# Routed sums of 48 row tiles on GpSimd instead of VectorE, with the last segment's first unit moved ahead

## What is computed

```python
x = L0_attn_a_x
x = x + _L0_attn_a_ref(_layernorm(x), ...)        # recurrence over 512 steps, 16 heads
x = x + _L0_ffn_ref(_layernorm(x), ...)           # experts
x = x + _L0_attn_b_ref(_layernorm(x), ...)        # causal attention
x = x + _L0_ffn_ref(_layernorm(x), ...)           # experts, same weights

# recurrence, one step for all sequences and heads
Sk = einsum('bhde,bhe->bhd', Sm, k_t)
Sm = Sm + beta_t[..., None] * einsum('bhd,bhe->bhde', v_t - Sk, k_t)
o_t = einsum('bhde,bhe->bhd', Sm, q_t)

# experts
scores = sigmoid(xt @ gate_w.T)
_, idx = lax.top_k(scores + gate_b, 4)
w = take_along_axis(scores, idx); w = w / sum(w) * 2.5
y = sum over the four chosen experts e of  w_e * (silu_and_mul(xt @ w13_e.T) @ w2_e.T)
y = y + silu_and_mul(xt @ w13_s.T) @ w2_s.T       # shared expert
```

## Time and profile before

| | us |
|---|---|
| median of 3 executions | 5779.35 |
| lowest and highest | 5775.86 and 5791.94 |
| the profiled execution, its own time | 5783.49 |
| the profiled execution, its span from first to last instruction | 5782.3 |

### The profile page before, as it was taken

The page is one execution under the profiler, slowest core; times in us unless marked ns, Lnnn a source line. Parts: engine busy times, 40 slices in busy tenths (PEclk is TensorE's granted clock), DMA queues, the critical chain, the costliest instruction groups (busy, mean ns, idle before and its releaser), DMA issues.

```text
span 5782.3 us, 71376 instructions
## 1 busy us (share of the span) xinstructions
PE 3420.9 (59%) x20276; PEld 2403.0 (42%) x20372; DVE 4123.7 (71%) x10439; ACT 1976.3 (34%) x4743; POOL 1764.7 (31%) x2760
## 2 busy tenths in 40 slices
PE   6312053663436533263548878876788778877664
PEld 3101031452315422152435555543565555545554
DVE  1999989999899988998356656665566556654333
ACT  3111021231213311031236545644555545544232
POOL 1010014303461133403352233235211433244523
PEclk8655576796668866697779999987999989988887
DMA  1210001462215421363532334311233323333776
GB/s 48 114 40 7 0 20 48 136 173 67 67 57 172 140 64 55 113 189 114 154 110 75 99 121 126 95 54 65 79 90 90 115 89 117 113 99 121 244 226 200
DMA packets 429265, 593.40 MB, mean 103 GB/s; under 512 B 57680, under 2 KB 304080, under 8 KB 428752
## 3 DMA queue, kind: packets, MB, share of 16 engines
q1 hardware_dynamic: 379728, 454.55, 26.3%
q0 software_dynamic: 49152, 134.28, 7.0%
HBM read 378.89 MB, written 209.72 MB: 102 GB/s over the span
## 4 chain that ended last, share of the span: by engine, by line
DVE 41%; PE 30%; issue 11%; POOL 9%; ACT 4%; DMA 3%; SPq 2%; another core or an unknown queue 1%; DVEq 0%; ACTq 0%; POOLq 0%
PE psum L1020 5%; DVE rec L1084 5%; DVE rec L1086 4%; DVE skb L1089 4%; DVE rec L1097 4%; DVE rec L1100 4%; POOL xbuck L1669 4%; DVE region L1092 3%; PE psum L930 3%; PE psum L878 3%; PE psum L1028 3%; DVE psum L1202 2%; DVE acc L1371 2%; POOL yg L1679 2%; PE psum L918 2%
## 5 line engine op out<-in xcount | busy, mean ns | idle before, releaser
L1020 PE MATMUL psum<-xgT,w 128*128 128x128 f32 x5376 | 798.9, 296 | 105.1 <-issue 57.9
L1679 POOL DMA_INDIRECT yg<-ybuck,words x512 | 529.6, 1034 | 988.1 <-issue 641.2
L1020 PEld LDWEIGHTS psum<-xgT,w 128*128 128x128 f32 x5376 | 729.2, 209 | 160.2 <-issue 123.2
L1028 PE MATMUL psum<-w_w2T,hid 128*128 x1344 | 475.0, 438 | 360.1 <-DVE hid L1353 227.0
L1202 DVE CUSTOM_DVE_ANT_0 psum<-psum,xo 128x128 f32<-128x128 f32 (+3 forms) x1024 | 473.7, 520 | 224.5 <-PE psum L899 204.5
L1669 POOL DMA_INDIRECT xbuck<-srow,words x512 | 521.9, 1019 | 152.3 <-issue 128.9
L810 PE MATMUL psum<-w_ident,xn 128*128 128x128 f32 x512 | 105.8, 343 | 773.5 <-ACT xn L1388 767.8
L1516 ACT ACTIVATE region<-psum 128x512 f32<-128x512 f32 (+3 forms) x1024 | 412.0, 443 | 348.4 <-PE psum L918 313.7
L1551 ACT ACTIVATE xgT<-psum 128x256 f32<-128x256 f32 x672 | 257.1, 383 | 760.7 <-PE psum L1010 709.2
L1650 POOL TENSOR_SCALAR_AFFINE_SELECT region<-region 128x128 f32<-128x128 f32 x1024 | 288.8, 300 | 670.5 <-ACT region L1516 656.2
L1038 DVE SCALAR_TENSOR_TENSOR sil<-sil,psum 128x128 f32<-128x128 f32 (+1 forms) x472 | 139.4, 295 | 448.9 <-ACT sil L1560 366.2
(11 more groups left out here) (201 smaller groups left out, 7576.4 us busy)
## 6 DMA issues: line engine op xcount, KB each, us to landing
w<-in_w13T SPq DMA_DIRECT2D x672, 256.0 KB
xg<-xbuck SPq DMA_DIRECT2D x672, 128.0 KB
ybuck<-yrow SPq DMA_DIRECT2D x672, 128.0 KB
xbuck<-x SPq DMA_DIRECT2D x40, 512.0 KB, 5.3
x_scratch<-res SPq DMA_DIRECT2D x64, 256.0 KB
acc<-x_scratch SPq DMA_DIRECT2D x128, 128.0 KB
xbuck<-srow,words POOLq DMA_INDIRECT x512
yg<-ybuck,words POOLq DMA_INDIRECT x512
```

The source lines that it names most:

```text
L1020: o = e.matmul(psum[:, mi, half], w13[I % 3][:, k, half], xgT[I % 2][:, k, :], start=(k == 0), stop=(k == 1), skip_group_check=True)
L1028: o = e.matmul(psum[:, mi, 0:D], hid[hi][:, 0:128], w2T[:, bass.ds(expert.pop(I), 1), :].rearrange("p a b -> p (a b)"), start=True, stop=True)
L1679: e.indirect_dma_start(yg[y % 5], None, ybuck[g % 2][0:TILES_OF[g] * 128, :], bass.IndirectOffsetOnAxis(ap=posu[g % 2][:, J - ROWS0[g], k: ...
```

## The change

POOL_SUMS is 48: for row tiles J under 48, y_sum is made on GpSimd and not on VectorE. [...] The semaphores `ysum` and the store are as before. The stage second_fill is new: GpSimd's part of second_setup now stands behind the scatter of group 3; the other engines' part stays. Behind the scan, unit 12's four row tiles come first, ahead of the other three units'; then `heads` goes on beside the other units' rows, and a head waits in the list until its own unit's rows are put. VectorE's first sum of tile 48 waits for `ysum`.

```diff
@@ -37,6 +37,8 @@
 
 LIGHT = 0.35
 HEAD_RATE, TILE_RATE, SUM_RATE, PROJECT_RATE = 0.6, 0.5, 0.2, 0.15
+
+POOL_SUMS = 48
 SCATTER, SPACE = 1.3, 4
 PHASE_RATE = {LIGHT: 0.32, 1: 0.32, 2: 0.2, 3: 0.04, 4: 0.3}
 
@@ -460,6 +462,8 @@
                     yield LIGHT
                 if b // 4 < NQ - 1:
                     yield from first_rows(b // 4, b % 4)
+                while b < NB and b not in added:
+                    yield LIGHT
                 yield from head(b)
             while g >= 2 and g - 2 not in summed:
                 yield LIGHT
@@ -475,6 +479,8 @@
                     for _ in range(SPACE):
                         yield LIGHT
             filled.add(g)
+            if UNIT0[g + 1] == NB - 3:
+                put("second_fill")
 
     def tiles():
         for g in range(NG):
@@ -585,11 +591,14 @@
     for i in range(4):
         xo.give(2 + i, "bred", 32)
     rows = [Strand(first_rows(NQ - 1, n)) for n in range(4)]
+    while not rows[0].done:
+        for t in rows[0:1] + streams[1:]:
+            t.step()
+    turned.add(NQ - 1)
     while not all(t.done for t in rows):
-        for t in rows + streams[1:]:
+        for t in streams + rows:
             t.step()
     put("second_setup")
-    turned.add(NQ - 1)
 
     norms = {}
 
@@ -1360,13 +1369,15 @@
                                        ALU.mult).then_inc(s["tg"], 1)
             elif name == "y_sum":
                 g, J = u
+                if J < POOL_SUMS:
+                    continue
                 a, j = acc[J % 2], J - ROWS0[g]
                 dv.wait_ge(s[f"ai{J % 2}"], 16 * (J // 2) + 16)
                 dv.wait_ge(s["rv"], RV0[g + 1])
                 for k in range(4):
                     y = 4 * J + k
                     dv.wait_ge(s[f"yg{y % 5}"], 16 * (y // 5) + 16)
-                    if k:
+                    if k or J == POOL_SUMS:
                         dv.wait_ge(s["ysum"], y)
                     e.scalar_tensor_tensor(a, yg[y % 5], ck[g % 2][:, j, k:k + 1], a, ALU.mult,
                                            ALU.add).then_inc(s["ysum"], 1)
@@ -1617,7 +1628,7 @@
                 r, q, n, j, oi, of, v = u
                 po.wait_ge(s[f"xo{oi}"], v)
                 e.tensor_tensor(xo[oi], xo[oi], boA[:, :], ALU.add).then_inc(s["rb"], 1)
-            elif name == "second_setup":
+            elif name == "second_fill":
                 po.wait_ge(s["oadd"], 64)
                 po.wait_ge(s["d_b"], 112)
                 e.tensor_copy(sel4, sel432).then_inc(s["bset"], 1)
@@ -1680,6 +1691,25 @@
                         yg[y % 5], None, ybuck[g % 2][0:TILES_OF[g] * 128, :],
                         bass.IndirectOffsetOnAxis(ap=posu[g % 2][:, J - ROWS0[g], k:k + 1],
                                                   axis=0)).then_inc(s[f"yg{y % 5}"], 16)
+
+            elif name == "y_sum":
+                g, J = u
+                if J >= POOL_SUMS:
+                    continue
+                a, j = acc[J % 2], J - ROWS0[g]
+                po.wait_ge(s[f"ai{J % 2}"], 16 * (J // 2) + 16)
+                po.wait_ge(s["rv"], RV0[g + 1])
+                for k in range(4):
+                    y = 4 * J + k
+                    po.wait_ge(s[f"yg{y % 5}"], 16 * (y // 5) + 16)
+                    e.tensor_scalar(yg[y % 5], yg[y % 5], ck[g % 2][:, j, k:k + 1], None,
+                                    ALU.mult).then_inc(s["yw"], 1)
+                for k in range(4):
+                    y = 4 * J + k
+                    po.wait_ge(s["yw"], y + 1)
+                    if k:
+                        po.wait_ge(s["ysum"], y)
+                    e.tensor_tensor(a, yg[y % 5], a, ALU.add).then_inc(s["ysum"], 1)
 
     def sync():
         sp = Eng(nc.sync)
```

## The result

The changed kernel takes 5926.68 us (5919.86 to 5930.68), 1.0248 times the kernel before [1.0232, 1.0263]. The forecast of 5863 had the sign and the places right and not quite 60% of the size: +147 us between the two profiled executions (spans 5929.4 and 5782.3), +84 forecast. The median lies 1.7 us above the range's upper end of 5925; the ratio times 5779.35, 5923 us, lies just inside it. Either way the forecast's own band, 5805 to 5905, was left.

What follows compares the result with a forecast made beforehand. VectorE was taken to set the pace in the scans, GpSimd between scan and attention. +16 + 17 - 7 + 58 = +84 on the median of 5779.35 gave 5863 us; range of 8 in 10, 5770 to 5925.

Steps and rivals of the forecast that it cites:

- VectorE's waits for xo in the first stretch: Sign, third scan (1389 to 1578 us): these waits grow from 8.9 to over 25 us.
- the row right behind an addition: Sign, behind the last scan: unit 12's first row comes some 150 us after scan's end, not 94, right behind an addition.
- rival 4: Behind the scan: unit 12's head, not GpSimd, comes last; tail +37, 5842 us; chance 0.62 shared with the forecast.
- 1: Rival, scans: GpSimd isn't the pace and costs VectorE nothing; -77, tail +40, 5742 us; chance 0.11.
- 2: Rival, scans: VectorE stays the pace at 1.5 us a tile; -23, tail +40, 5796 us; chance 0.14.
- 1.5 forecast: Scans: a tile's eight GpSimd instructions cost VectorE 1.5 us, leaving it 0.65 of its 2.15 us gain.
- rival 3: Scans: each of the eight instructions holds VectorE for its whole length; +106, tail +58, 5943 us; chance 0.13.
- The scans, +33 forecast: Third and fourth scan, stretches with unit work: +16 (205 against 189 us) and +17 (191 against 174).
- GpSimd's queue in the scan: Scans: sums at 7.2 us a tile make GpSimd's queue the pace, a third of load waits kept; +16 and +17.
- Behind the scan, +58 forecast: Scan's end to unit 12's first row: twelve tiles at 11.1 us on GpSimd put that row at 2852, not 2793.40.
- Unit 12 first and the later fill: Behind the scan: head done by 2830, before GpSimd is free; fill's 5 us covered by 20.98 us of GpSimd idling.
- The 11 tiles beside nothing: Ends of the last three scans and between them: VectorE keeps 0.65 us a tile, -7 us.

Runs made afterwards that it cites:

- e7: Changed kernel with the bias added by TensorE and no bias addition on GpSimd: 1.0114 times the kernel before, 5841 us.
- e12: e8 with the addition ending the scores of units 0 to 11, and its constant columns, made by VectorE: 0.9969 times the kernel before.
- e8: Changed kernel with GpSimd sums in the scans alone, two-op products, bias by TensorE, old order and fill behind the scan: 1.0017 times the kernel before, 5792 us.
- e4: Kernel before with two idle GpSimd instructions beside each first-scan step: additions 5.08 us a step against 4.54, products 4.15 against 4.13 and 4.17 against 4.16.
- e6: Changed kernel with a second operation (plus a column of zeros) in GpSimd's products: 1.0195 times the kernel before.
- e1: Changed kernel with all sums on VectorE again, unit 12 first and the later fill kept: 1.0014 times the kernel before.
- e10: Kernel before with the bias by TensorE and GpSimd's fill behind the scatter of group 3: 0.9960 times the kernel before.
- e5: Kernel before with runs of idle GpSimd instructions in the first scan, not timed to VectorE's steps: additions cost 0.29 us each, two-op products 0.14, sums 1.5 a tile.

## Why the prediction came out as it did

**Right.** Slower, and by GpSimd's queue. VectorE's waits for xo in the first stretch (25.1, over 25 forecast), the row right behind an addition, and GpSimd and not the head last: routing ends at 2909.9, 23 us ahead of the row, so rival 4 didn't happen. Rivals 1 to 3 fell: the scans and the stretch behind all grew by more than forecast, so GpSimd was the pace, against 1 and 2, and a step's instructions on VectorE grew by 0.22 and 0.40 us, 36 and 35 steps, 22 us for 24 tiles, 0.9 a tile (1.5 forecast, 5.1 in rival 3). VectorE did get its gain: in the unit parts of the two scans its busy time fell from 199.2 to 186.2 us and from 191.1 to 186.1; it spent it waiting.

**Luck.** The range reaches beyond 5905 only to take in the lower part of rival 3, and rival 3 didn't happen. That the ratio falls inside says nothing for the mechanism; the terms below were too small by 63 us.

**The scans, +33 forecast, +61 measured.** The step that failed is **GpSimd's queue in the scan**. Its busy time came out near (164.68 and 157.00; 84.25 + 93.6 = 178, one tile too many, since only twelve ran in the first stretch, and 70.59 + 86.4 = 157), but by two errors that cancel: a tile took 7.9 and 8.3 us, not 7.2, and the gathers less than before (44 of 1059 ns, 46.6 us, where the earlier trace rows have 47 of 1189, 55.9). What was mis-sized are its waits: a third of the loads' 38.1 and 63.3 us was kept, 13 and 21; 27.6 stayed inside the first stretch and 27.7 in the second. I let a late GpSimd find its loads landed, and named SyncE's stores only in passing; but a sum makes its own store late, and that the next load, and a late VectorE is late with its res and with the buffers that SyncE waits for. A tile's products were 1077 and 1101 ns where the 16 of the earlier trace rows had 860; those 16, like the row at 2799.67, have two operations. GpSimd's groups by line in the first stretch of the changed kernel (busy, mean ns), which answer to the earlier trace rows:

```profile
L1705 POOL TENSOR_SCALAR yg<-yg,words 128x256 f32<-128x256 f32 x48 | 51.2, 1077 | 0.0
...
L1712 POOL TENSOR_TENSOR acc<-yg,acc 128x256 f32<-128x256 f32 x48 | 39.1, 815 | 5.2
```

And the rout waits were seen in no term: the scores' addition stands in the same queue as the bias. e7 shows the bias's place in that queue as a cause, and e12, on e8's shorter queue, that of the scores, each by taking its instruction out. That the store in front of the load is a link between them is read from the time lines; a store on another queue was not tried. One reading of the prediction was half right: of VectorE's 8.9 us before, 4.5 stood behind a gather, and 4.4 behind GpSimd's own wait for a load.

**Behind the scan, +58 forecast, +75.5 measured.** A tile took 11.84 us (12.57 from the gather at 2803.01 to the next tile's, less a bias addition of 0.73) and not 11.1: 9 us for twelve, because a product took 0.905 us in place of 0.56 + 0.04, while four additions took 3.31 in place of 3.76. The 0.56 came from the row at 2799.67, a product with two operations; e4 and e6 show that the single one is the longer. Loads waited for, 10.5 us and not 5: 5.5. Tile 36 starts 5 us later against the scan's end. Bias additions at 0.73 give 2 back. (9 + 5.5 + 5 - 2 = 17.5.)

**Unit 12 first and the later fill**, costed at nothing: +6 to the row (e1; in the changed kernel it lies within the 75.5), and the cover named for the fill, 20.98 us of idle GpSimd, lay behind the next unit's norm and not ahead of it (e10). **The 11 tiles beside nothing**, -7: the gaps between the scans are 23.5 and 23.1 us, 22.4 and 23.9 before, and the second scan takes 638.1, 638.7 before; nothing came back. The rest of the 147, some 11 us, lies ahead of the third scan and behind the first row, and no experiment gives it a cause.

## What to carry to other kernels

An engine whose busy share is half can still be full: ask of each instruction that is moved which later ones of that queue are waited for, and follow the wait through every queue, the stores' and loads' included, until it comes back to the engine that was to be relieved. Here 2 us off VectorE put 8 into a queue that VectorE waits for. What gained a little was to make that queue shorter: the bias by TensorE alone takes 18 us off the kernel before (0.9969 [0.9958, 0.9980]). Price an instruction by a row of its own form, op for op: 0.55 and 0.92 us differ here by one operand.

## What the runs showed of the hardware

A GpSimd product 128x256 by a column takes 0.92 us with one operation and 0.55 with a second, in place or elsewhere (shortest durations in e4 and e5; 0.905 and 0.54 each behind the scan). Beside VectorE's scan an addition of two tensors on GpSimd costs VectorE 0.27 to 0.29 us (e4, e5), a one-op product at most 0.1, a two-op product next to nothing at a step's start and 0.14 in e5; reductions on VectorE (0.67) pay nothing and cost nothing (in e5 all 19 two-op products that met reductions alone kept their 0.55 us). The Trainium skill (GPSIMD Engine Reference, Key points) states that the two engines share their SBUF interfaces and that VectorE instructions with two SBUF inputs contend; the 0.69 us that became 1.1 to 1.2, and the 0.67 that stayed, agree. The 0.69 of L1098, which stayed too, shows that the price also hangs on which of the two starts first; what else sets it was not separated.
